# Attention: VectorE turns, inverts and spreads a group's softmax sums inside their bank

## The reference

```python
q, k, v = x @ wq, x @ wk, x @ wv          # 16 query heads, 4 key/value heads of 32
q, k = rope(q), rope(k)
attn = einsum('bhqd,bhkd->bhqk', q, k) / sqrt(32)
attn = softmax(where(mask, -inf, attn), axis=-1)
out = einsum('bhqk,bhkd->bhqd', attn, v)
x = x + out @ wo
```

## Time and profile before

| | |
|---|---|
| median of 3 runs | 1289.16 us (1288.6 to 1290.42) |
| the profiled execution | 1283.76 us, span 1282.5 us |
| attention stage | about 420 to 1020 us of the span |
| TensorE's mean granted clock | 0.988 |
| busy in the span | PE 1197.2 us, DVE 893.1, ACT 665.8, POOL 598.1 |

### The profile page before, as it was taken

How to read it: one execution, slowest core, us unless ns; L and a number is a source line. 1 busy time by engine, 2 the same in 40 slices (tenths; PEclk the granted TensorE clock), 3 DMA queues, 4 the chain that set the end, 5 groups by cost and what they waited for, 6 DMA issues and landing times.

```text
span 1282.5 us, 22107 instructions
## 1 busy us (share of the span) xinstructions
PE 1197.2 (93%) x7413; PEld 778.6 (61%) x7413; DVE 893.1 (70%) x2100; ACT 665.8 (52%) x1321; POOL 598.1 (47%) x496
## 2 busy tenths in 40 slices
PE   4899999999998999999999999999999978999996
PEld 3678888858776554445545455545544346777774
DVE  7767777779997665476577677587763666666664
ACT  2545455436555554265466556366567853444442
POOL 4844444313210111001437556455773373888886
PEclk9899999999999999999999999999999999999999
DMA  9923333565530022013445845655743263666665
GB/s 331 365 92 108 112 111 108 172 178 108 98 60 16 21 69 35 1 59 78 98 127 138 165 100 106 192 133 146 152 100 67 84 240 72 106 100 102 101 102 79
DMA packets 68557, 148.52 MB, mean 116 GB/s; under 512 B 8832, under 2 KB 29312, under 8 KB 64448
## 3 DMA queue, kind: packets, MB, share of 16 engines
q0 software_dynamic: 35184, 93.34, 34.1%
q1 hardware_dynamic: 33264, 53.77, 12.1%
HBM read 81.28 MB, written 33.55 MB: 90 GB/s over the span
## 4 chain that ended last, share of the span: by engine, by line
PE 61%; DVE 15%; DMA 10%; issue 6%; POOL 4%; ACT 4%; SPq 0%; POOLq 0%; DVEq 0%; ACTq 0%
PE bank L839 10%; PE bank L1636 10%; PE bank L1648 9%; PE bank L997 8%; PE bank L862 5%; PE bank L1703 4%; PE bank L1666 4%; DMA XG<-xn,TK 3%; DMA out<-Y,DI 3%; POOL out L789 3%; DVE bank L1012 2%; DMA CD<-P 2%; DVE PM L1010 2%; PE bank L821 2%; PE bank L1398 2%
## 5 line engine op out<-in xcount | busy, mean ns | idle before, releaser
L1755 ACT ACTIVATE P<-bank 128x512 f32<-128x512 f32 (+3 forms) x640 | 304.2, 537 | 255.4 <-PE bank L1636 246.2
L1010 DVE TENSOR_REDUCE PM<-bank 128x1 f32<-128x512 f32 x384 | 252.9, 685 | 79.7 <-PE bank L997 78.9
L1636 PE MATMUL bank<-Qs,Ks 98*128 98x512 f32 (+3 forms) x640 | 242.8, 409 | 5.1 <-ACT P L1755 2.8
L997 PE MATMUL bank<-Ks,Qs 96*128 96x512 f32 (+3 forms) x640 | 233.4, 386 | 8.9 <-DVE PM L1012 5.3
L1636 PEld LDWEIGHTS bank<-Qs,Ks 98*128 98x128 f32 x640 | 117.2, 190 | 141.5 <-ACT P L1755 65.3
L1814 POOL TENSOR_SCALAR_AFFINE_SELECT P<-P 128x512 f32<-128x512 f32 x64 | 43.5, 694 | 283.4 <-ACT P L1755 283.4
L1012 DVE CUSTOM_DVE_ANT_0 bank<-bank,KB 128x128 f32<-128x128 f32 (+3 forms) x256 | 124.5, 497 | 51.4 <-PE bank L997 50.7
L1648 PE MATMUL bank<-P,V 128*32 128x512 f32 (+3 forms) x1280 | 151.3, 544 | 4.1 <-POOL P L1814 4.1
L997 PEld LDWEIGHTS bank<-Ks,Qs 96*128 96x128 f32 x640 | 121.7, 191 | 54.1 <-DVE PM L1010 17.0
L1828 POOL TENSOR_TENSOR CH<-CH,P 128x512 f32<-128x512 f32 x108 | 139.5, 1446 | 13.3 <-ACT P L1755 12.7
L789 POOL DMA_INDIRECT out<-Y,DI x78 | 126.3, 1619 | 38.2 <-issue 28.0
(11 more groups left out here) (195 smaller groups left out, 1977.7 us busy)
## 6 DMA issues: line engine op xcount, KB each, us to landing
CD<-P POOLq DMA_DIRECT2D x17, 1024.0 KB, 7.3
xn<-XN SPq DMA_DIRECT2D x8, 1024.0 KB, 6.9
WR<-L_ffn_w POOLq DMA_DIRECT2D x16, 512.0 KB, 15.1
XO<-y POOLq DMA_DIRECT2D x8, 1024.0 KB, 9.6
WR<-L_ffn_w SPq DMA_DIRECT2D x16, 512.0 KB, 7.7
CD<-P SPq DMA_DIRECT2D x7, 1024.0 KB, 5.2
CD<-CH POOLq DMA_DIRECT2D x7, 1024.0 KB, 7.5
XA<-y POOLq DMA_DIRECT2D x24, 256.0 KB, 4.1
```

Of the source, the lines that this page charges most:

```text
L997: pe.matmul(bk(g, bank)[:, 0:n], g.Qs[b][0:96, G % 4 * 4 + h, c * P:c * P + P], g.Ks[0:96, G % 4, k * BQ:k * BQ + n], start=True, stop=Tru ...
L1010: dve.tensor_reduce(dst, bk(g, bank)[:, 0:n], AX.X, ALU.max).then_inc(s(f"free{bank}"), 1)
L1636: pe.matmul(bk(g, bank)[:, o:BQ], g.Ks[0:98, G % 4, k * P:k * P + P], g.Qs[G // 4][0:98, G % 4 * 4 + j, o:BQ], start=True, stop=True).then ...
L1755: act.activation(a.P4[buffer_of(n)][:, j, o:BQ], bk(g, score_bank(g, i))[:, o:BQ], ACT.Exp, scale=scale).then_inc(s("exp"), 1)
```

## The change

At `out`, VectorE itself turns bank 4 in 32x32 blocks into `SM`. A block there has one query's sum in each row, so one column for each block is enough. `recip`, one score step on, takes the reciprocal of those 16 columns into `R`, now 128x16, and turns `R`, each element repeated 32 times, back in blocks into bank 4. That is the layout of `OT`. `even`, three steps on, is VectorE's product alone. ScalarE's copy and TensorE's `tsum` and `even` are gone, and the two take no bank of the ring. The next group's first L1666 and the lending of bank 4 wait for semaphore `even`, which the product raises.

```diff
-                    put(at + 4, ("tsum", G0))
-                    put(at + 8, ("even", G0))
+                    put(at + 1, ("recip", G0))
+                    put(at + 3, ("even", G0))
...
-        if step[0] in ("top", "proj", "tsum", "even", "found"):
+        if step[0] in ("top", "proj", "found"):
             ring.take(step)
...
             if fresh and G:
-                pe.wait_ge(s("sm"), G)
+                pe.wait_ge(s("even"), G)
...
         if kind == "even" and step[1] in g.lent:
-            pe.wait_ge(s("sm"), step[1] + 1)
+            pe.wait_ge(s("even"), step[1] + 1)
...
         act.copy(a.OTs[b % 2][:, G % 4, :], bk(g, 3)).then_inc(s("oT"), 1)
-        act.wait_ge(s("sum"), SUMMED[LAST[G]] + 1)
-        act_shared(g, ("tsum", G))
-        act.copy(g.SM[:], bk(g, 4)).then_inc(s("sm"), 1)
...
+    def sums(G):
+
+        before = shared_before(g, ("sums", G))
+        if before[0] == "found":
+            dve.wait_ge(s("md"), 16 * before[1] + 16)
+        if G:
+            dve.wait_ge(s("even"), G)
+        dve.wait_ge(s("sum"), SUMMED[LAST[G]] + 1)
+        dve.transpose(g.SM[:], bk(g, 4)).then_inc(dv.sem, 1)
+        turned[G] = dv.up()
+
+    def recip(G):
+        dve.wait_ge(dv.sem, turned[G])
+        dve.reciprocal(a.R[:], g.SM[:].rearrange("p (c j) -> p c j", j=32)[:, :, 0]).then_inc(dv.sem, 1)
+        dve.wait_ge(dv.sem, dv.up())
+        dve.transpose(bk(g, 4).rearrange("p (c j) -> p c j", j=32),
+                      a.R[:].unsqueeze(2).to_broadcast([P, 16, 32])).then_inc(dv.sem, 1)
+        spread[G] = dv.up()
+
+    def even(G):
+        dve.wait_ge(dv.sem, spread[G])
+        dve.wait_ge(s("oT"), G + 1)
+        o = a.OTs[G // 4 % 2][:, G % 4, :]
+        if G < 15:
+            dve.tensor_tensor(o, o, bk(g, 4), ALU.mult).then_inc(s("even"), 1)
+            return
...
+        elif kind == "out":
+            sums(step[1])
+        elif kind == "recip":
+            recip(step[1])
```

More of the change, by code:

```diff
@@ L270, in memory @@
     a.WO = t("WO", [P, 4, D])
-    a.R = t("R", [P, 4, 4])
+    a.R = t("R", [P, 16])
     low = Area(nc, Q0, Q1)
@@ L1066, in act_found, with shared_before @@
     act.wait_ge(s(f"full{bank}"), use + 1)
-    act_shared(g, ("found", G))
+    before = shared_before(g, ("found", G))
+    if before and before[0] == "found":
+        act.wait_ge(s("md"), 16 * before[1] + 16)
+    elif before:
+        act.wait_ge(s("even"), before[1] + 1)
     act.copy(g.mT[:], bk(g, bank)[0:8, :]).then_inc(s(f"free{bank}"), 1)
-def act_shared(g, key):
+def shared_before(g, key):
     at = g.shared.index(key)
[L1074 to L1081, removed]
+    return g.shared[at - 1] if at else None
 def sp_found(g, G):
@@ L1538, in attend_plan @@
             plan += due
-            free = free or any(step[0] == "tsum" for step in due)
+            free = free or any(step[0] == "even" for step in due)
             if turned:
@@ L1571, in attend_plan @@
     assert not later and not extra and not ahead, (later, extra, len(ahead))
-    plan += [("weigh", len(TILES) - 1), ("out", 15), ("up1", 4), ("split1", 0), ("split1", 1), ("split1", 2), ("split1", 3), ("tsum", 15), ("even", 15)]
+    plan += [("weigh", len(TILES) - 1), ("out", 15), ("up1", 4), ("split1", 0), ("split1", 1), ("split1", 2), ("split1", 3), ("recip", 15), ("even", 15)]
     for c in range(4):
@@ L1600, in attend_plan @@
         if step[0] == "out":
-            g.shared.append(("tsum", step[1]))
+            g.shared.append(("sums", step[1]))
         elif step[0] == "foundcopy":
@@ L1668, in weigh @@
             ins.then_inc(s("sum"), 1)
[L1670 to L1685, removed]
     def proj(key):
@@ L1691, in proj @@
             pe.wait_ge(s("wo"), 16)
[L1692 to L1695, removed]
         if b == 3:
@@ L1698, in proj @@
         if b == 3 and c < 3:
+            pe.wait_ge(s("even"), 15)
             pe.wait_ge(s("norm"), c + 1)
         else:
-            pe.wait_ge(s(f"free{b0}"), u0 + 1)
+            pe.wait_ge(s("even"), 4 * b + 4)
         for k in range(4):
@@ L1717, in pe_attend @@
             pe_found(g, step[1])
[L1718 to L1721, removed]
         elif kind == "proj":
@@ L1867, in dve_attend @@
 def dve_attend(g):
-    s, dve, a = g.s, g.nc.vector, g.a
+    s, dve, dv, a = g.s, g.nc.vector, g.dv, g.a
+    turned, spread = {}, {}
     all_projected(g, dve.wait_ge)
@@ L1914, in even @@
         if G < 15:
-            dve.tensor_tensor(o, o, bk(g, bank), ALU.mult).then_inc(s(f"free{bank}"), 1)
+            dve.tensor_tensor(o, o, bk(g, 4), ALU.mult).then_inc(s("even"), 1)
             return
@@ L1918, in even @@
             v = slice(c * P, c * P + P)
-            ins = dve.tensor_tensor(o[:, v], o[:, v], bk(g, bank)[:, v], ALU.mult)
-            ins.then_inc(s("norm") if c < 3 else s(f"free{bank}"), 1)
+            dve.tensor_tensor(o[:, v], o[:, v], bk(g, 4)[:, v], ALU.mult).then_inc(s("norm") if c < 3 else s("even"), 1)
     for step in g.plan:
@@ L1930, in dve_attend @@
                 pair(step[1])
-        elif kind == "tsum":
-            tsum(step)
+        elif kind == "out":
+            sums(step[1])
+        elif kind == "recip":
+            recip(step[1])
         elif kind == "even":
-            even(step)
+            even(step[1])
         elif kind == "proj":
```

## The result

The changed kernel takes 1303.86 us in the median (1298.57 to 1308.23), beside 1289.35 us for the kernel before on the same chip. The ratio is 1.0127, 95% interval 1.0093 to 1.0162: slower by some 15 us. Forecast were 1297.5 us and a range of 1288 to 1308. The profiled execution took 1300.80 us (span 1299.5), 17.0 more than that of before (1283.76, span 1282.5). The clock's mean over the span fell from 0.988 to 0.974.

A forecast was written before the change was run, and what follows sets the result against it. TensorE was taken to bound the attention stage. Terms without the clock summed to +0.2 us, clock falls added 8.5, so +8.7 on the median of 1289.16: forecast 1297.5 us, range 1288 to 1308.

The forecast's parts named there:

- The removed work: TensorE's transposes and narrow matmuls, 1.46 us a group, gone in groups 0 to 13: -20.4 us; waits before them: -2.1.
- The turns: Two VectorE turns of 128x512 a group, taken at 0.61 us between starts.
- Cheap turns: Rival: VectorE's turns take 0.42 us, waits shrink too short to bring the clock down, 1281 to 1286 us; chance 0.06.
- dear turns: Rival: VectorE's second turn needs two passes each, 16.6 us over 13 chains and more clock falls, 1304 to 1318; chance 0.12.
- The six waits at lending: Ends of groups 7 to 12: TensorE waits for VectorE's product before the next score matmul, 16.3 us in all.
- The waits at the first sum: Groups 0 to 6: the next group's first sum waits for the product, 0.5 to 1.9 us each, 8.8 together.
- The ring: Maxima held once by turns in groups 13 and 14, +0.7 us; fewer ring steps and an earlier fourth bank, -1.5.
- each restart: TensorE's first matmul after each of 13 waits costs about 0.1 us more, 1.3 us in all.
- The end of the stage: Group 15, ScalarE the bound: 1.8 us gained before it; after the last sum a shorter chain saves 1.1 us.
- The sum without the clock: All terms for work, waits, ring, restarts and stage end added: +0.2 us, the gain eaten by the waits.
- The clock: TensorE's clock falls after waits: four falls for the six long, one for the seven shorter, 1.7 us each, 8.5 us.
- The rival that the clock stays: The waits come but TensorE's clock does not fall: 1287.5 to 1291 us, not tellably slower; chance 0.20.

The follow-up runs named there:

- e9: e8 with TensorE's removed transposes and narrow matmuls put back on constants for groups 0 to 14, result unused; 1290.97 us, ratio 1.0032.
- e1: The changed kernel with bank 4 lent to the ring five score steps later; 1282.33 us, ratio 0.9962.
- e3: e2 with TensorE's wait for the product at the lending of bank 4 put back; 1315.37 us, ratio 1.0211.
- e4: The changed kernel with twelve matmuls on constants in front of the six waits at lending; 1291.5 us, ratio 1.0034.
- e7: e5 with its second turn done twice in each group; 1301.64 us, ratio 1.0121.
- e5: e2, but the last group's second turn and product use bank 4 again; 1276.55 us, ratio 0.9925.
- e8: e5 with reciprocal and second turn one score step later, product and lending three later; 1270.95 us, ratio 0.9891.
- e12: The same kernel as e8, timed again without a change; 1270.09 us, ratio 0.9865.
- e2: The changed kernel with the second turn written to SBUF, lending and next first sum waiting for the first turn only; 1288.37 us, ratio 1.0006.

## Why the prediction was right, and where not

**The removed work** (-20.4 and -2.1). Right in kind: e9 puts it at 1.2 to 1.4 us a group, where I had 1.46.

**The turns** (0.61 between starts). Right: they take 712 and 727 ns, 0.64 and 0.63 us from start to next start in group 11. Cheap turns and dear turns both fall with that. For the second turn, which reads an element 32 times, the rule on adjacent pairs that the prediction quoted from the Trainium skill would have been 0.35 us more; it took 15 ns more than the first, so here a repeated element does not pay it.

**The six waits at lending** (16.3). Right, 15.4: the term stood at 3.2, 3.1, 2.7, 2.4, 2.8 and 2.1 us for groups 7 to 12, and the trace has 2.74, 2.85, 2.67, 2.39, 2.64 and 2.08. e1 and e3 show by two routes that they come from the wait for the product, and cost their length and more. The closeness is in part luck. In group 11 the first turn starts 0.52 us after the last sum's end, where I had it start at once, and the product ends 4.8 us after it, not 4.5; but TensorE comes to the score 2.25 us after that end, not 1.7, for it had waited for a bank of the ring (0.26 us) on the way.

**The waits at the first sum** (8.8). Half as long: four of 1.07, 1.30, 0.54 and 1.16 us for groups 0 to 3 and none for 4 to 6, where the ring waits once in each for a maximum (0.53, 0.74 and 0.70 us). 6.0 us in all.

**The ring** (+0.7 in group 13, -1.5). Wrong in sign. Outside the removed steps, whose waits are in the -2.1, TensorE's waits for a maximum from 416 to 1000 us were 2.3 us before and are 7.1 after: +4.8, where the two terms gave -0.8. The three waits of groups 4 to 6 are part of that. No run shows the 0.1 us for each restart (+1.3) apart.

**The end of the stage** (-1.8 and -1.1). The lag behind before was 15.9 us at the end of group 13 and 14.2 at that of group 15: -1.8. It was 13.1 at the first projection: -1.1. Both right.

**The sum without the clock** (+0.2). The 17.0 us of the profiled executions less 15.3 of clock loss leave +1.7. That this is near is luck in part: the first sums were 4.7 us too dear, and the ring 5.6 us too cheap.

**The clock** (+8.5) is the term that was mis-sized. The step "I count four falls for them and one for the seven shorter" was of the right kind, and five of the six places did lose clock. But two of them lost 3.4 us and not 1.7, the shorter waits lost some as well (the stretch from 550 us, 0.83), and two stretches outside the waits lost 5.3 us more. The added loss was 15.3 us. How much of that part belongs to the change stays open. The start of the stage lost between 0 and 6.8 us in the 14 profiled executions, without a pattern in what was changed. Over all executions the clock is 0.972 against 0.986 to 0.988, so that the fall itself is no accident of one profile. The medians, 14.5 us apart, are a little nearer to each other than the profiles. The forecast of 1297.5 us is also 0.4 us under its own sum: 1289.16 + 8.7 is 1297.9.

**The rival that the clock stays** falls in both ways: with waits, the clock fell (five of the six stretches below 0.92), and with the waits filled (e4) it did not, but for one. What the prediction quoted from "TensorE: Matmul & The Clock Gate" of the Trainium skill on brief idling between bursts agrees in part. It is no rule for each idle time: the one of 2.08 us at 892.48 left the clock at 1.00, as the one of 1.33 us did in the earlier trace rows, and after the one of 0.74 us at 552.84 it was at half from 554 to 556 us. Nor does any run show a length of wait below which the clock stays, as the rival of the cheap turns supposed.

What I had not seen is what VectorE's added load does by way of the ring. I priced it at 0.7 us (group 13). e7 shows 7.5 us of waits for one more turn a group, and twice as much in clock loss.

## What to carry to other kernels

Where an engine is the bound, moving work off it pays only if what replaces the work is not waited for: here a loss of 16 us became a gain of 10 as soon as the bank was free after the first turn (e5), and of 14 to 17 with the chain spread over the tile (e8, e12). Lay out the new chain with all that is queued between its links, and free the shared buffer at the first link that allows it, not at the last. Count on TensorE's idle time to cost more than its length (15.4 us of waits cost 27 in e3, 7.5 us cost 25 in e7; there is no fixed factor), and read the clock of the stretches around each wait before blaming the wait alone. Take the clock of several executions for that: two profiles of one kernel (e8 and e12) differ by 3.4 us of clock loss. And before a VectorE step is moved, look at what GpSimd does at its new place.

## What the runs showed of the hardware

- A VectorE product of two SBUF operands, 128x128 in float32, took 4.4 us beside GpSimd's TENSOR_TENSOR of 128x2048 (4.5 us each), and 0.28 us with one operand in PSUM beside the same work (e2 and e5). In groups 0 to 14 of e2 GpSimd's TENSOR_TENSOR ran beside two of the products only, from near their end on, and none took longer. In e8 a product of 128x512 took 4.78 us beside several of GpSimd's 128x512, and 0.68 alone.
- VectorE's 32x32 turn of 128x512 in float32 takes 712 ns from PSUM to SBUF, 727 ns from a repeated element to PSUM and 711 ns from one to SBUF (e2).
- Matmuls on constants in an idle time of 2.5 us kept TensorE's clock up at five of six places and took 12 us off the kernel (e4), though they compute nothing.
